# Softmax row bookkeeping per four heads instead of two, factor product on GpSimd, value products released by the copied outputs

## The chip, the cores and the metric

The kernel runs on one core of one Trainium2 chip. The metric is the device time of one execution in microseconds (us). The core's engines are TensorE (PE: matmuls and transposes, with PEld for its weight loads), VectorE (DVE), ScalarE (ACT), GpSimd (POOL) and SyncE (SP), which here issues every DMA. Each engine works through its own queue in order. Semaphores join them.

## The reference

```python
h = jnp.maximum(_layernorm(x, axis=-1), 0.0)          # x: (32, 256, 512) f32
q, k, v = (split_heads(h @ W.T) for W in (Wq, Wk, Wv))  # 16 heads of 32
a = jnp.einsum('bhnd,bhmd->bhnm', q, k) * scale + (adj + adj)[:, None]
row_nonzero = jnp.any(a != 0, axis=-1, keepdims=True)
a = jnp.where(row_nonzero, a, -jnp.inf)
p = jax.nn.softmax(a, axis=-1)
p = jnp.where(jnp.isnan(p), 0.0, p)                   # a row of zeros gives 0
o = jnp.einsum('bhnm,bhmd->bhnd', p, v)
out = x + o.transpose(0, 2, 1, 3).reshape(B, N, D) @ Wo.T
```

A row of scores that is zero throughout gives an output of zero, and all others are divided by their sum of exponentials. The "row bookkeeping" of the title is that test, the reciprocal of the sum, the product of both (the factor) and the multiplication of the head's output by it.

## The kernel before

The 32 batches are worked through one after another: `body` is written out for batch 0 and the last one, and a hardware loop does batches 1 to 30. Within a batch every engine runs over the 16 heads `hh`, in its own hand-written order, and everything is in split precision (a high and a low part).

A head `hh` passes through these steps:

- `scores` (PE, L395) writes 256 rows by 256 columns into one of three PSUM banks, three heads ahead.
- `shift` (DVE, L765) adds the adjacency, turns the sign, writes `minus` and gathers each row's bound in the last column of `bounds`. It runs two heads ahead.
- `exponentials` (ACT, L586) writes `probs`. `transpose_probs` (PE, L406) turns them. `high_probs` (ACT, L597) and `low_probs` (DVE, L774) write the two halves `pT_hi` and `pT_lo`.
- `values` (PE, L427 and L428) multiplies them with `v_parts` into the single bank `o_ps`: two heads share it, and at every even `hh` PE does both heads of the pair before. One column of ones in `v_parts` gives the row sums.

The row bookkeeping goes by pairs of heads:

- `fold` (POOL, L912 and L918) adds the halves of `minus` twice, to 64 columns a row in `bounds`, so that DVE's reduction is short.
- `any_nonzero` (DVE, at every odd `hh`, for the pair before): a reduction over `bounds` (`some`, L783) and the reciprocal of the sums, in the bank `o_ps` itself (L787).
- `factors` (DVE, L796): the factor, from `some` and `o_ps`. It stands behind the `take` calls of that head and ahead of `low_probs`.
- `copy_outputs` (ACT, L575) copies the bank to `o_raw`.
- `divide` (POOL, L887 and L892): adds the high and low outputs, and multiplies by the factor into `o`.
- `values` of the next pair waits for `factor_ready`, since the factor is read from the bank that it overwrites.

Into these steps the projections are laid as jobs (the table `JOBS`, PE L331, L346, L371). `("h", n, 1)` are the transposes of the next batch's normalised tokens (h0 at `hh` 4, h1 at 5), `("qk", n, 1)` and `("v", n, ..)` their projections, `("o", 1, -1)` at `hh` 3 the transposes of the last half of the previous batch's outputs, and `("y", n, -1)` the output projection (y0 from `hh` 4). Jobs alternate between two PSUM banks. A job starts when the job that had its bank before is "taken": copied out by ACT (high part) and DVE (low part), L551 to L564 and L729 to L747.

What stands around the change in a batch: at `hh` 0 DVE does `moments_of(b + 1)` (L665, L670) behind `low_probs`. At `hh` 1 its order is `shift` of head 3, `any_nonzero` and `factors` of the previous batch's last pair, `low_probs` of head 1. At `hh` 1 POOL's order is

```python
fold(b, 1, ...)           # waits for shift of head 3
divide(b - 1, PAIRS - 1)  # the previous batch's last pair
normalise(b + 1, False)   # L867, L869, L872, L880; then h_ready
```

and the transposes h0 at `hh` 4 wait for `h_ready` in PE's queue, with the job y0 behind them. The transposes o1 at `hh` 3 wait for `o_ready`, which `divide` gives. SP stores `y` and loads the next tokens and the adjacency, and copies `qk_parts` to `qk_stack`.

Of the kernel before, what the change touches and what calls it, by code (L numbers as in the profile page):

```python
# [5 lines left out]
ALU = mybir.AluOpType  # L6
# [7 lines left out]
P = 128  # L14
# [62 lines left out]
def attention_block(nc, x, adj, wq, wk, wv, wo_t, out):  # L77
# [9 lines left out]
    ONES, LOW = HD, HD + 1  # L87
    FREE = 3 * HD
    PAIRS = HEADS // 2

    UNTOP = 1.0 / (W_TOP * H_TOP)
# [9 lines left out]
    with ExitStack() as ctx:  # L101
# [40 lines left out]
        fold1 = [sb(f"fold1_{i}", [P, 2 * NT, N // 2]) for i in range(2)]  # L142
        some = [sb(f"some{i}", [P, 2 * NT]) for i in range(2)]
        factor = [sb(f"factor{i}", [P, 2 * NT]) for i in range(2)]

        o_raw = [sb(f"o_raw{i}", [P, 2 * NT, VW - 1]) for i in range(2)]
        probs = [sb(f"probs{i}", [P, NT, N]) for i in range(2)]
# [21 lines left out]
        o_ps = psum("o_ps")  # L169
        o_sums = o_ps[:, :].rearrange("p (q c) -> p q c", c=P)  # L170
        job_ps = [psum(f"job_ps{i}") for i in range(2)] + [s_ps[0]]
# [29 lines left out]
        some_ready, rcp_ready = sem("some_ready"), sem("rcp_ready")  # L201
        factor_ready, o_ready = sem("factor_ready"), sem("o_ready")
        o_added = sem("o_added")
# [109 lines left out]
        def _(pe):  # L313
# [23 lines left out]
            def job(kind, n, d, start, stop, b):  # L337
# [28 lines left out]
                elif kind == "o":  # L366

                    if start == 0:
                        pe.wait_ge(o_ready, (b + d) * PAIRS + 4 * (n + 1))
                    for k, t in [divmod(i, NT) for i in range(start, stop)]:  # L370
# [39 lines left out]
            def values(b, hh, early):  # L410
# [92 lines left out]
        def _(act):  # L503
# [125 lines left out]
            def body(b, first, last):  # L629
                for hh in range(HEADS):  # L630
                    if hh % 2:

                        if hh > 1:
                            copy_outputs(b, hh // 2 - 1, first and hh < 7)
                        elif not first:
                            copy_outputs(b - 1, PAIRS - 1, False)
# [23 lines left out]
        def _(dve):  # L660
# [88 lines left out]

            def shift(b, hh, early):  # L750
# [28 lines left out]

            def any_nonzero(b, pair):  # L780

                dve.wait_ge(folded2, b * PAIRS + (pair + 1))
                nc.vector.tensor_reduce(some[pair % 2][:, :], bounds[:, pair % 4, :, :], AX_X, ALU.max,  # L783
                                        apply_absolute_value=True).then_inc(some_ready, 1)

                dve.wait_ge(o_copied, b * PAIRS + (pair + 1))
                nc.vector.reciprocal(o_sums[:, :, FREE], o_sums[:, :, ONES]).then_inc(rcp_ready, 1)  # L787

            def factors(b, pair, early):

                dve.wait_ge(some_ready, b * PAIRS + (pair + 1))
                dve.wait_ge(rcp_ready, b * PAIRS + (pair + 1))
                if not early:

                    dve.wait_ge(o_ready, b * PAIRS + (pair - 1))
# [31 lines left out]
            def body(b, first, last):  # L827
                for hh in range(HEADS):
                    if hh + 2 < HEADS:
                        shift(b, hh + 2, first and hh + 2 < 4)  # L830
                    elif not last:
                        shift(b + 1, hh + 2 - HEADS, False)

                    pair = None
                    if hh % 2 and not (first and hh == 1):
                        pair = (b, hh // 2 - 1) if hh > 1 else (b - 1, PAIRS - 1)
                        any_nonzero(*pair)
                    for kind, n, d in ended_before(hh, first, last):
                        take(kind, n, b + d)
                    if pair:  # L840
                        factors(*pair, first and hh < 6)
# [7 lines left out]
            body(B - 1, False, True)  # L849
            any_nonzero(B - 1, PAIRS - 1)  # L850
            factors(B - 1, PAIRS - 1, False)
            take("o", 1, B - 1)

        @block.gpsimd
        def _(pool):
# [27 lines left out]

            def divide(b, pair):

                pool.wait_ge(factor_ready, b * PAIRS + (pair + 1))
                nc.gpsimd.tensor_tensor(o_raw[pair % 2][:, :, 0:HD], o_raw[pair % 2][:, :, 0:HD],  # L887
                                        o_raw[pair % 2][:, :, LOW:LOW + HD], ALU.add).then_inc(o_added, 1)

                pool.wait_ge(o_added, b * PAIRS + (pair + 1))  # L890
                col = 2 * pair * HD
                nc.gpsimd.tensor_tensor(  # L892
                    o[:, :, col:col + 2 * HD].rearrange("p t (h d) -> p h t d", h=2),
                    o_raw[pair % 2][:, :, 0:HD].rearrange("p (h t) d -> p h t d", h=2),
                    factor[pair % 2][:, :].rearrange("p (h t) -> p h t", h=2).unsqueeze(3).to_broadcast([P, 2, NT, HD]),
                    ALU.mult).then_inc(o_ready, 1)
# [9 lines left out]
            def fold(b, pair, early):  # L906
# [8 lines left out]
                if not early:  # L915

                    pool.wait_ge(some_ready, b * PAIRS + (pair - 1))
                nc.gpsimd.tensor_tensor(f2, f1[:, :, 0:N // 4], f1[:, :, N // 4:N // 2],  # L918
# [34 lines left out]
            def body(b, first, last):  # L953
                for hh in range(HEADS):
                    if hh % 2 == 1:
                        if hh + 2 < HEADS:
                            fold(b, hh // 2 + 1, first and hh // 2 + 1 < 2)
# [17 lines left out]
            body(B - 1, False, True)  # L975
            divide(B - 1, PAIRS - 1)
            for t in range(NT):
# [28 lines left out]
```

## Time and profile before

| | |
|---|---|
| median of 3 runs | 1286.47 us (1285.94 to 1288.19) |
| the profiled execution | 1286.69 us, span 1284.9 us |
| busy: PE, PEld | 1246.0 us (97%), 1110.2 us (86%) |
| busy: DVE, ACT, POOL | 1111.5 us (87%), 1052.2 us (82%), 898.3 us (70%) |
| mean granted TensorE clock | 0.994 of full speed |

The span runs from the first to the last instruction of the profiled execution. The busy times are sums over it. PE's matmuls are pipelined, so that the time printed for one is longer than the distance from its start to the next one's; a wait of PE is read from those distances and from the idle time printed for PEld. A batch repeats itself nearly to the nanosecond, so one batch in the middle of the span shows what all of the loop do.

### The profile page before, as it was taken

The page shows a single profiled execution, that of the slowest core. Times are in us where ns is not written, and L with a number is a line of the kernel's source. Part 1 is how long each engine was busy: PE and PEld are TensorE (multiplying, and loading weights), DVE is VectorE, ACT ScalarE, POOL GpSimd, SP SyncE. Part 2 cuts the span into 40 slices and gives each one's busy share as a digit, 9 for nine tenths or more (in the row PEclk, how much of TensorE's full clock was granted, in tenths as well). Part 3 has the DMA queues.
Part 4 walks back from the last instruction along what each step waited for, and adds up shares of the span by engine and source line. Part 5 has one row for each costly group of instructions (what it writes and reads, how often), then busy time and mean ns, then how long its engine had stood idle before and what let it go on. Part 6 is the DMA issues. An engine that isn't in the chain of part 4 may idle for free. (4 is left out here: it accounts for less than half of the span.)

```text
span 1284.9 us, 43970 instructions
## 1 busy us (share of the span) xinstructions
PE 1246.0 (97%) x13104; PEld 1110.2 (86%) x13104; DVE 1111.5 (87%) x4003; ACT 1052.2 (82%) x2429; POOL 898.3 (70%) x1272
## 2 busy tenths in 40 slices
PE   4899999999999999999999999999999999999996
PEld 4788988888988888888888888888888888988885
DVE  5798888888888888888888888888889898889884
ACT  4788888888888888888888888888888888888884
POOL 6676677776677776677776677776677776677765
PEclk9999999999999999999999999999999999999998
DMA  6344554554554554554554554554554554554551
GB/s 216 96 110 126 135 123 126 135 143 112 137 122 124 137 140 113 139 122 122 139 134 117 141 122 120 141 132 116 144 122 117 144 131 115 147 122 115 130 123 51
DMA packets 90772, 163.88 MB, mean 128 GB/s; under 512 B 14976, under 2 KB 23168, under 8 KB 90752
## 3 DMA queue, kind: packets, MB, share of 16 engines
q1 hardware_dynamic: 90752, 163.64, 49.1%
q8 instruction: 10, 0.16, 0.1%
q14 instruction: 10, 0.08, 0.0%
HBM read 46.14 MB, written 16.78 MB: 49 GB/s over the span
## 5 line engine op out<-in xcount | busy, mean ns | idle before, releaser
L912 POOL TENSOR_TENSOR fold<-minus 128x512 f32<-128x512 f32 x256 | 326.9, 1277 | 299.2 <-DVE bounds L765 299.2
L586 ACT ACTIVATE probs<-minus,bounds 128x256 f32<-128x256 f32 x1024 | 459.8, 499 | 26.6 <-DVE bounds L765 25.0
L774 DVE TENSOR_TENSOR pT_lo<-pT_ps,pT_hi 128x512 f16<-128x512 f32 x512 | 351.2, 686 | 63.2 <-ACT pT_hi L597 60.0
L765 DVE CUSTOM_DVE_ANT_0 minus<-s_ps,adj_now 128x256 f32<-128x256 f32 x1024 | 388.6, 416 | 7.7 <-ACT probs L586 4.7
L597 ACT ACTIVATE pT_hi<-pT_ps 128x512 f16<-128x512 f32 x512 | 304.9, 596 | 109.6 <-PE pT_ps L406 107.9
L406 PE MATMUL pT_ps<-ident,probs 128*128 128x128 f32 x2048 | 307.5, 273 | 1.7 <-ACT probs L586 1.6
L331 PE MATMUL job_ps<-hT_hi,w_hi 128*128 128x256 f16 x1024 | 280.5, 274 | 0.8 <-DVE hT_lo L729 0.8
L331 PE MATMUL job_ps<-hT_hi,w_lo 128*128 128x256 f16 x1024 | 279.2, 273 | 0.0
L331 PE MATMUL job_ps<-hT_lo,w_hi 128*128 128x256 f16 x1024 | 279.1, 273 | 0.0
L406 PEld LDWEIGHTS pT_ps<-ident,probs 128*128 128x128 f32 x2048 | 241.8, 141 | 19.0 <-ACT probs L586 2.5
L395 PE MATMUL s_ps<-qk_stack 96*128 96x256 f32 x1024 | 246.8, 323 | 0.0
L918 POOL TENSOR_TENSOR bounds<-fold 128x256 f32<-128x256 f32 x256 | 187.8, 734 | 24.9 <-POOL fold L912 9.5
L427 PE MATMUL o_ps<-v_parts,pT_hi 128*128 128x65 f16 x2048 | 157.1, 192 | 8.2 <-DVE pT_lo L774 7.7
L395 PEld LDWEIGHTS s_ps<-qk_stack 96*128 96x128 f32 x1024 | 154.6, 191 | 0.3 <-DMA qk_stack<-qk_parts 0.2
L428 PE MATMUL o_ps<-v_parts,pT_lo 128*128 128x33 f16 x2048 | 150.2, 178 | 0.0
L427 PEld LDWEIGHTS o_ps<-v_parts,pT_hi 128*128 128x128 f16 x2048 | 123.8, 97 | 24.0 <-DVE pT_lo L774 11.6
L331 PE MATMUL job_ps<-w_hi,hT_hi 128*128 128x256 f16 x512 | 140.7, 275 | 1.8 <-DVE qk_parts L737 1.8
L331 PE MATMUL job_ps<-w_lo,hT_hi 128*128 128x256 f16 x512 | 139.8, 273 | 0.0
L331 PE MATMUL job_ps<-w_hi,hT_lo 128*128 128x256 f16 x512 | 139.6, 273 | 0.0
L428 PEld LDWEIGHTS o_ps<-v_parts,pT_lo 128*128 128x128 f16 x2048 | 126.8, 96 | 0.0
L892 POOL TENSOR_TENSOR o<-o_raw,factor 128x128 f32<-128x128 f32 x256 | 103.1, 403 | 20.1
L331 PEld LDWEIGHTS job_ps<-hT_hi,w_hi 128*128 128x128 f16 x1024 | 99.8, 97 | 16.0 <-issue 0.9
(79 smaller groups left out, 2264.3 us busy)
## 6 DMA issues: line engine op xcount, KB each, us to landing
qk_stack<-qk_parts SPq DMA_DIRECT2D x768, 128.0 KB, 2.3
x_in<-x SPq DMA_DIRECT2D x32, 512.0 KB, 3.4
x_res<-x SPq DMA_DIRECT2D x32, 512.0 KB, 3.7
out<-y SPq DMA_DIRECT2D x64, 256.0 KB, 2.1
adj_in<-adj SPq DMA_DIRECT2D x32, 256.0 KB, 3.5
w_in<-wq SPq DMA_DIRECT2D x2, 512.0 KB, 6.1
w_in<-wk SPq DMA_DIRECT2D x2, 512.0 KB, 7.9
w_in<-wv SPq DMA_DIRECT2D x2, 512.0 KB, 9.9
```

The costliest lines, as they stand in the source:

```text
L331: end = nc.tensor.matmul(dst, lhs[a](k), rhs[c](k), start=i == 0, stop=i == len(terms) - 1)
L395: end = nc.tensor.matmul(s_ps[SCORE_BANK[hh]][:, t * N:(t + 1) * N], stack[:, 0, t * P:(t + 1) * P], stack[:, 1, :], start=True, stop=True)
L406: end = nc.tensor.transpose(pT_ps[hh % 2][:, m * N + t * P:m * N + (t + 1) * P], probs[hh % 2][:, t, m * P:(m + 1) * P], ident[:, :])
L427: nc.tensor.matmul(ps[:, 0:LOW + HD], hi, v[:, 0:LOW + HD], start=m == 0, stop=False)
L428: end = nc.tensor.matmul(ps[:, 0:HD + 1], lo, v[:, 0:HD + 1], start=False, stop=m == NT - 1)
L586: end = nc.scalar.activation(probs[hh % 2][:, t, :], minus[hh // 2 % 2][:, hh % 2, t, :], ACT.Exp, bias=bounds[:, hh // 2 % 4, 2 * (hh % 2 ...
L597: nc.scalar.activation(pT_hi[hh % 4][:, :, :], pT_ps[hh % 2][:, :].rearrange("p (m n) -> p m n", m=NT), ACT.Copy).then_inc(pT_high, 1)
L765: end = nc.vector.tensor_tensor_reduce(out=minus[pair % 2][:, hh % 2, t, :], in0=s_ps[SCORE_BANK[hh]][:, t * N:(t + 1) * N], in1=adj_now[: ...
L774: nc.vector.tensor_tensor(pT_lo[hh % 4][:, :, :], pT_ps[hh % 2][:, :].rearrange("p (m n) -> p m n", m=NT), pT_hi[hh % 4][:, :, :], ALU.sub ...
L892: nc.gpsimd.tensor_tensor(o[:, :, col:col + 2 * HD].rearrange("p t (h d) -> p h t d", h=2), o_raw[pair % 2][:, :, 0:HD].rearrange("p (h t) ...
L912: nc.gpsimd.tensor_tensor(f1[:, :, :], src[:, :, 0:N // 2], src[:, :, N // 2:N], ALU.add).then_inc(folded1, 1)
L918: nc.gpsimd.tensor_tensor(f2, f1[:, :, 0:N // 4], f1[:, :, N // 4:N // 2], ALU.add).then_inc(folded2, 1)
```

## The change

The bookkeeping goes by four heads (a "quad"). `any_nonzero` runs at `hh` 1, 5, 9 and 13: one reduction over the four heads' bounds and one reciprocal, read from `o_raw` in SBUF and written to a tile of its own. `factors` is gone from DVE. GpSimd's `divide`, at the same four `hh`, turns `some` into a mask, multiplies it with the reciprocals, adds the high and low outputs of four heads and multiplies them by the factor: four instructions for four heads, where four of the old ones served them too. `values` waits for `o_copied` instead of `factor_ready`. Semaphore counts follow, and `shift` has one wait more at every fourth head.

```diff
-        factor = [sb(f"factor{i}", [P, 2 * NT]) for i in range(2)]
-        o_raw = [sb(f"o_raw{i}", [P, 2 * NT, VW - 1]) for i in range(2)]
+        row_scale = [sb(f"row_scale{i}", [P, 4 * NT]) for i in range(2)]
+        mask = sb("mask", [P, 4 * NT])
+        factor = sb("factor", [P, 4 * NT])
+        o_raw = [sb(f"o_raw{i}", [P, 2, 2 * NT, VW - 1]) for i in range(2)]
 # PE: job "o", values
-                        pe.wait_ge(o_ready, (b + d) * PAIRS + 4 * (n + 1))
+                        pe.wait_ge(o_ready, (b + d) * QUADS + 2 * (n + 1))
-                    pe.wait_ge(factor_ready, b * PAIRS + hh // 2)
+                    pe.wait_ge(o_copied, b * PAIRS + hh // 2)
 # ACT: copy_outputs
-                    act.wait_ge(o_ready, b * PAIRS + (pair - 1))
-                nc.scalar.activation(o_raw[pair % 2][:, :, :],
+                    act.wait_ge(o_ready, b * QUADS + (pair // 2 - 1))
+                nc.scalar.activation(o_raw[pair // 2 % 2][:, pair % 2, :, :],
 # DVE: shift
+                    if hh % 4 == 0 and not fresh:
+                        dve.wait_ge(some_ready, b * QUADS + (pair // 2 - 1))
 # DVE
-            def any_nonzero(b, pair):
-                dve.wait_ge(folded2, b * PAIRS + (pair + 1))
-                nc.vector.tensor_reduce(some[pair % 2][:, :], bounds[:, pair % 4, :, :], AX_X, ALU.max, ...)
-                dve.wait_ge(o_copied, b * PAIRS + (pair + 1))
-                nc.vector.reciprocal(o_sums[:, :, FREE], o_sums[:, :, ONES]).then_inc(rcp_ready, 1)
-            def factors(b, pair, early):
...
-                nc.vector.scalar_tensor_tensor(factor[pair % 2][:, :], some[pair % 2][:, :], 0.0,
-                                               o_sums[:, :, FREE], ALU.not_equal, ALU.mult).then_inc(factor_ready, 1)
+            def any_nonzero(b, quad, early=False):
+                dve.wait_ge(folded2, b * PAIRS + 2 * (quad + 1))
+                if not early:
+                    dve.wait_ge(factor_ready, b * QUADS + (quad - 1))
+                nc.vector.tensor_reduce(some[quad % 2][:, :], bounds[:, 2 * (quad % 2):2 * (quad % 2) + 2, :, :].rearrange(
+                    "p r q c -> p (r q) c"), AX_X, ALU.max, apply_absolute_value=True).then_inc(some_ready, 1)
+                dve.wait_ge(o_copied, b * PAIRS + 2 * (quad + 1))
+                nc.vector.reciprocal(row_scale[quad % 2][:, :], o_raw[quad % 2][:, :, :, ONES]...).then_inc(rcp_ready, 1)
 # DVE: body
-                    if hh % 2 and not (first and hh == 1):
+                    if hh % 4 == 1 and not (first and hh == 1):
 # POOL
-            def divide(b, pair):
...
+            def divide(b, quad):
+                pool.wait_ge(some_ready, b * QUADS + (quad + 1))
+                settled(pool, "pool")
+                nc.gpsimd.tensor_scalar(mask[:, :], some[quad % 2][:, :], 0.0, 1.0, ALU.is_gt, ALU.mult
+                                        ).then_inc(masked, 1)
+                pool.wait_ge(masked, b * QUADS + (quad + 1))
+                pool.wait_ge(rcp_ready, b * QUADS + (quad + 1))
+                nc.gpsimd.tensor_tensor(factor[:, :], mask[:, :], row_scale[quad % 2][:, :], ALU.mult
+                                        ).then_inc(factor_ready, 1)
+                raw = o_raw[quad % 2]
+                nc.gpsimd.tensor_tensor(raw[:, :, :, 0:HD], raw[:, :, :, 0:HD], raw[:, :, :, LOW:LOW + HD],
+                                        ALU.add).then_inc(o_added, 1)
+                pool.wait_ge(factor_ready, b * QUADS + (quad + 1))
+                pool.wait_ge(o_added, b * QUADS + (quad + 1))
+                nc.gpsimd.tensor_tensor(o[...four heads...], raw[...], factor[...].to_broadcast([P, 4, NT, HD]),
+                    ALU.mult).then_inc(o_ready, 1)
 # POOL: body
-                        if hh > 1:
-                            divide(b, hh // 2 - 1)
-                        elif not first:
-                            divide(b - 1, PAIRS - 1)
+                        if hh in (5, 9, 13):
+                            divide(b, hh // 4 - 1)
+                        elif hh == 1 and not first:
+                            divide(b - 1, QUADS - 1)
```

## Rows read from the trace of the kernel before

**Rows 1.** The page, part 1: busy us, share of the span, instructions.
```profile
PE 1246.0 (97%) x13104; PEld 1110.2 (86%) x13104; DVE 1111.5 (87%) x4003; ACT 1052.2 (82%) x2429; POOL 898.3 (70%) x1272
```

**Rows 2.** The waits of PEld: total us, times, longest us.
```profile
PEld o_ps L427 <- DVE pT_lo L774: 11.6, 36, 1.0
PEld job_ps L331 <- DVE qk_parts L737: 8.4, 32, 1.7
PEld job_ps L331 <- DVE oT_lo L747: 8.0, 33, 1.8
PEld job_ps L371 <- issue: 6.2, 30, 0.2
```

**Rows 3.** The timeline of PE and PEld, heads 2 to 4: start us, us.
```profile
585.91 0.20 PE L427 MATMUL o_ps<-v_parts,pT_hi 128*128 128x65 f16 x1 [0.20 <-DVE pT_lo L774]
...
624.11 0.19 PE L427 MATMUL o_ps<-v_parts,pT_hi 128*128 128x65 f16 x1
624.52 0.20 PE L427 MATMUL o_ps<-v_parts,pT_hi 128*128 128x65 f16 x1 [0.20 <-DVE pT_lo L774]
...
627.83 0.27 PE L331 MATMUL job_ps<-w_hi,hT_lo 128*128 128x256 f16 x1
628.04 0.65 PE L371 MATMUL job_ps<-ident,o 128*128 128x128 f32 x4
629.72 0.65 PE L346 MATMUL job_ps<-ident,h 128*128 128x128 f32 x4
...
630.31 0.19 PEld L331 LDWEIGHTS job_ps<-wo_hi,oT_hi 128*128 128x128 f32 x1 [0.18 <-DVE oT_lo L747]
```

**Rows 4.** The timeline of DVE in the same batch.
```profile
620.54 1.27 DVE L665 BATCH_NORM_STATS2 stats<-x_in 128x6 f32<-128x512 f32 x2
...
622.95 0.42 DVE L783 TENSOR_REDUCE some<-bounds 128x4 f32<-128x260 f32 x1
623.29 0.18 DVE L787 RECIPROCAL o_ps<-o_ps 128x4 f32<-128x4 f32 x1
...
623.77 0.69 DVE L774 TENSOR_TENSOR pT_lo<-pT_ps,pT_hi 128x512 f16<-128x512 f32 x1
...
627.41 0.18 DVE L787 RECIPROCAL o_ps<-o_ps 128x4 f32<-128x4 f32 x1
627.50 0.41 DVE L743 SCALAR_TENSOR_TENSOR v_parts<-job_ps,v_parts 128x256 f16<-128x256 f32 x1
...
629.51 0.68 DVE L747 TENSOR_TENSOR oT_lo<-job_ps,oT_hi 128x512 fp32r<-128x512 f32 x1
```

**Rows 5.** The timeline of ACT there.
```profile
628.73 0.60 ACT L564 ACTIVATE oT_hi<-job_ps 128x512 fp32r<-128x512 f32 x1 [0.16 <-PE job_ps L371]
```

**Rows 6.** The timeline of POOL there, from the fold at head 1.
```profile
623.11 1.27 POOL L912 TENSOR_TENSOR fold<-minus 128x512 f32<-128x512 f32 x1 [2.95 <-DVE bounds L765]
624.46 0.72 POOL L918 TENSOR_TENSOR bounds<-fold 128x256 f32<-128x256 f32 x1
625.14 0.41 POOL L887 TENSOR_TENSOR o_raw<-o_raw 128x128 f32<-128x128 f32 x1
...
626.12 0.23 POOL L867 TENSOR_SCALAR minus_mean<-mean_var 128x2 f32<-128x2 f32 x1
...
627.73 1.52 POOL L880 TENSOR_SCALAR h<-x_in,minus_mean,rstd 128x512 f32<-128x512 f32 x2 [0.30 <-POOL rstd L872]
```

**Rows 7.** Groups of instructions by line: busy us, mean ns, idle before.
```profile
L892 POOL TENSOR_TENSOR o<-o_raw,factor 128x128 f32<-128x128 f32 x256 | 103.1, 403 | 20.1
...
L796 DVE SCALAR_TENSOR_TENSOR factor<-some,o_ps 128x4 f32<-128x4 f32 x256 | 39.0, 152 | 18.8 <-DVE o_ps L787 5.9
...
L677 DVE TENSOR_REDUCE w_scale<-w_in 128x2 f32<-128x1024 f32 x3 | 3.6, 1208 | 2.0 <-DMA w_in<-wk 2.0
```

**Rows 8.** The chain that ended last: start us, us, what.
```profile
1271.27 0.20 DVE o_ps L787
...
1272.73 1.13 PE s_ps L371 x4
```

More of the change, by code:

```diff
@@ L87, in attention_block @@
     ONES, LOW = HD, HD + 1
-    FREE = 3 * HD
     PAIRS = HEADS // 2
+    QUADS = HEADS // 4
     UNTOP = 1.0 / (W_TOP * H_TOP)
@@ L142, in attention_block @@
         fold1 = [sb(f"fold1_{i}", [P, 2 * NT, N // 2]) for i in range(2)]
-        some = [sb(f"some{i}", [P, 2 * NT]) for i in range(2)]
-        factor = [sb(f"factor{i}", [P, 2 * NT]) for i in range(2)]
-        o_raw = [sb(f"o_raw{i}", [P, 2 * NT, VW - 1]) for i in range(2)]
+        some = [sb(f"some{i}", [P, 4 * NT]) for i in range(2)]
+        row_scale = [sb(f"row_scale{i}", [P, 4 * NT]) for i in range(2)]
+        mask = sb("mask", [P, 4 * NT])
+        factor = sb("factor", [P, 4 * NT])
+        o_raw = [sb(f"o_raw{i}", [P, 2, 2 * NT, VW - 1]) for i in range(2)]
         probs = [sb(f"probs{i}", [P, NT, N]) for i in range(2)]
@@ L169, in attention_block @@
         o_ps = psum("o_ps")
-        o_sums = o_ps[:, :].rearrange("p (q c) -> p q c", c=P)
         job_ps = [psum(f"job_ps{i}") for i in range(2)] + [s_ps[0]]
@@ L201, in attention_block @@
         some_ready, rcp_ready = sem("some_ready"), sem("rcp_ready")
-        factor_ready, o_ready = sem("factor_ready"), sem("o_ready")
+        masked, factor_ready, o_ready = sem("masked"), sem("factor_ready"), sem("o_ready")
         o_added = sem("o_added")
@@ L633, in body @@
                         if hh > 1:
-                            copy_outputs(b, hh // 2 - 1, first and hh < 7)
+                            copy_outputs(b, hh // 2 - 1, first and hh < 10)
                         elif not first:
@@ L748, in take, with shift @@
                                             oT_hi[:, 2 * n:2 * n + 2, :].bitcast(F32), ALU.subtract).then_inc(taken["o"], 1)
-            def shift(b, hh, early):
+            def shift(b, hh, early, fresh=False):
                 pair = hh // 2
@@ L775, in low_probs @@
                                         pT_hi[hh % 4][:, :, :], ALU.subtract).then_inc(pT_split, 1)
-            def any_nonzero(b, pair):
-                dve.wait_ge(folded2, b * PAIRS + (pair + 1))
-                nc.vector.tensor_reduce(some[pair % 2][:, :], bounds[:, pair % 4, :, :], AX_X, ALU.max,
-                                        apply_absolute_value=True).then_inc(some_ready, 1)
-                dve.wait_ge(o_copied, b * PAIRS + (pair + 1))
-                nc.vector.reciprocal(o_sums[:, :, FREE], o_sums[:, :, ONES]).then_inc(rcp_ready, 1)
-            def factors(b, pair, early):
-                dve.wait_ge(some_ready, b * PAIRS + (pair + 1))
-                dve.wait_ge(rcp_ready, b * PAIRS + (pair + 1))
-                if not early:
-                    dve.wait_ge(o_ready, b * PAIRS + (pair - 1))
-                nc.vector.scalar_tensor_tensor(factor[pair % 2][:, :], some[pair % 2][:, :], 0.0,
-                                               o_sums[:, :, FREE], ALU.not_equal, ALU.mult).then_inc(factor_ready, 1)
+            def any_nonzero(b, quad, early=False):
+                dve.wait_ge(folded2, b * PAIRS + 2 * (quad + 1))
+                if not early:
+                    dve.wait_ge(factor_ready, b * QUADS + (quad - 1))
+                nc.vector.tensor_reduce(some[quad % 2][:, :], bounds[:, 2 * (quad % 2):2 * (quad % 2) + 2, :, :].rearrange(
+                    "p r q c -> p (r q) c"), AX_X, ALU.max, apply_absolute_value=True).then_inc(some_ready, 1)
+                dve.wait_ge(o_copied, b * PAIRS + 2 * (quad + 1))
+                nc.vector.reciprocal(row_scale[quad % 2][:, :], o_raw[quad % 2][:, :, :, ONES].rearrange("p r q -> p (r q)")
+                                     ).then_inc(rcp_ready, 1)
             moments_of(0)
@@ L829, in body @@
                     if hh + 2 < HEADS:
-                        shift(b, hh + 2, first and hh + 2 < 4)
+                        shift(b, hh + 2, first and hh + 2 < 4, first and hh + 2 < 8)
                     elif not last:
                         shift(b + 1, hh + 2 - HEADS, False)
-                    pair = None
-                    if hh % 2 and not (first and hh == 1):
-                        pair = (b, hh // 2 - 1) if hh > 1 else (b - 1, PAIRS - 1)
-                        any_nonzero(*pair)
+                    if hh % 4 == 1 and not (first and hh == 1):
+                        any_nonzero(*((b, hh // 4 - 1) if hh > 1 else (b - 1, QUADS - 1)), first and hh < 12)
                     for kind, n, d in ended_before(hh, first, last):
                         take(kind, n, b + d)
-                    if pair:
-                        factors(*pair, first and hh < 6)
                     low_probs(b, hh, first and hh < 2)
@@ L849, in _ @@
             body(B - 1, False, True)
-            any_nonzero(B - 1, PAIRS - 1)
-            factors(B - 1, PAIRS - 1, False)
+            any_nonzero(B - 1, QUADS - 1)
             take("o", 1, B - 1)
@@ L882, in normalise @@
                 end.then_inc(h_ready, 1)
-            def divide(b, pair):
[L886 to L891, printed above, removed]
+            def divide(b, quad):
[12 more added lines that the diff above has]
+                pool.wait_ge(o_added, b * QUADS + (quad + 1))
+                col = 4 * quad * HD
                 nc.gpsimd.tensor_tensor(
-                    o[:, :, col:col + 2 * HD].rearrange("p t (h d) -> p h t d", h=2),
-                    o_raw[pair % 2][:, :, 0:HD].rearrange("p (h t) d -> p h t d", h=2),
-                    factor[pair % 2][:, :].rearrange("p (h t) -> p h t", h=2).unsqueeze(3).to_broadcast([P, 2, NT, HD]),
+                    o[:, :, col:col + 4 * HD].rearrange("p t (h d) -> p h t d", h=4),
+                    raw[:, :, :, 0:HD].rearrange("p r (h t) d -> p (r h) t d", h=2),
+                    factor[:, :].rearrange("p (h t) -> p h t", h=4).unsqueeze(3).to_broadcast([P, 4, NT, HD]),
                     ALU.mult).then_inc(o_ready, 1)
@@ L915, in fold @@
                 if not early:
-                    pool.wait_ge(some_ready, b * PAIRS + (pair - 1))
+                    pool.wait_ge(some_ready, b * QUADS + (pair // 2 - 1))
                 nc.gpsimd.tensor_tensor(f2, f1[:, :, 0:N // 4], f1[:, :, N // 4:N // 2],
@@ L956, in body @@
                         if hh + 2 < HEADS:
-                            fold(b, hh // 2 + 1, first and hh // 2 + 1 < 2)
+                            fold(b, hh // 2 + 1, first and hh // 2 + 1 < 4)
                         elif not last:
                             fold(b + 1, 0, False)
-                        if hh > 1:
-                            divide(b, hh // 2 - 1)
-                        elif not first:
-                            divide(b - 1, PAIRS - 1)
+                        if hh in (5, 9, 13):
+                            divide(b, hh // 4 - 1)
+                        elif hh == 1 and not first:
+                            divide(b - 1, QUADS - 1)
                     if not last and hh == 1:
@@ L975, in _ @@
             body(B - 1, False, True)
-            divide(B - 1, PAIRS - 1)
+            divide(B - 1, QUADS - 1)
             for t in range(NT):
```

## The prediction

> **What bounds the kernel.** I read the page's busy times first. PE is busy 97% of the span, and DVE with 87% and POOL with 70% are not near it [rows 1]. So work taken from DVE or added to POOL is worth nothing in itself; it counts only where PE waits for that engine. The list of waits comes next. In the loop PEld waits in four places only, about once in each batch: for DVE's low probabilities, for the low parts of a qk job, for the low part of oT, and once more ahead of the transposes L371, which the profile calls issue [rows 2]. I then read one batch engine by engine. Batches repeat every 38.61 us (624.52 less 585.91) [rows 3], and all four places lie between heads 2 and 4 of it, right after DVE has done the next batch's moments. There DVE is late: from the moments at 620.54 on it works nearly without a gap [rows 4]. Elsewhere PE waits for nobody.
>
> Two limits count in this stretch, and the change touches both. DVE releases PE at heads 2 to 4. POOL gives h_ready, for which the transposes L346 (h0) wait at head 4. POOL's L880 starts at 627.73 and takes 1.52, so h_ready comes at 629.25 [rows 6]. PE starts the transposes at 629.72 [rows 3]. No wait is printed there, because there is none: PE comes 0.47 us after h_ready. If I allow 0.05 us for a release to reach PE (the distances between a release and its start in this trace are of that size: low probabilities end at 623.77 + 0.69 = 624.46 and PE starts at 624.52 [rows 3, 4]), POOL has 0.42 us of slack in every batch. Nothing in the list of waits shows this number. It has to be worked out.
>
> **The change on DVE.** At head 1 the reduction grows from 260 to 520 columns. A slope from the rows: 417 ns at 260 (0.42) and 1208 ns at 1024, so 1.035 ns a column [rows 4, 7], so 0.27 us more. The reciprocal stays (four columns more, from SBUF in place of PSUM; I take the same 0.18). The factor goes with its wait: reciprocal to low probabilities was 623.77 - 623.29 = 0.48 [rows 4], and behind a reciprocal that nobody waits for the next instruction starts after 0.09 (627.41 to 627.50) [rows 4]. Net at head 1: 0.27 - 0.39 = -0.12 us. PE's first wait is 624.52 - 624.11 = 0.41 for a step of about 0.06, so it is about 0.35 long [rows 3], and it shortens by 0.12. The second (qk parts) stays as it is: DVE is earlier by 0.12 and so is PE.
>
> At head 3 DVE has no bookkeeping at all any more. It loses a reduction's step, a reciprocal's 0.09 and a factor, together at least 0.42 us ahead of taking the v job (L743 at 627.50) [rows 4]. The transposes L371 start 0.21 behind the last product where the products of that job step by 0.11; I read the missing 0.10 as a wait for L743, which ends at 627.91 and has the bank that they need, although the profile names nobody [rows 3, 4]. That 0.10 goes. The wait for the low part of oT (0.18 printed [rows 3]) goes nearly whole: ACT's high part would end at 628.73 + 0.60 = 629.33, less PE's own gain of 0.22 [rows 5], and DVE, which started L747 at 629.51 [rows 4], is free by then. So DVE's relief is worth at most 0.12 + 0.10 + 0.18 = 0.40 us a batch. The rest of what DVE saves (in a quad two factors, a reciprocal and a step) lies under PE's work and is worth nothing; the same holds for PE's new wait for o_copied, an earlier event than the old one and not among PE's waits, and for the extra wait in shift, on DVE's own result of an earlier head.
>
> **The change on POOL.** The old divide at head 1 occupies POOL from 625.14 to the start of L867 at 626.12: 0.98 us [rows 6]. It had half of the work that the new one has there, because the new divide is bunched: it comes at heads 1, 5, 9, 13 and does four heads. Behind it in POOL's queue stands normalise, and for that PE waits. The new divide step by step:
>
> - extra wait ahead of the mask: 0.05, my estimate;
> - mask, 8 columns: nearest row L867, 0.23 [rows 6];
> - factor, 8 columns, two inputs, behind the mask's own result. A dependent start takes 0.08 (623.11 + 1.27 to 624.46) and at most 0.30 where several waits stand ahead (the idle time printed for L880) [rows 6]. I take 0.12, then 0.23 again for the operation. From above it is bounded by L887's row of 128 columns, 0.41 [rows 6];
> - add, 256 columns: L887's 0.41 at 128 plus 128 columns at the slope between the folds, (1.27 - 0.72) / 256 = 2.1 ns [rows 6]: 0.68, started 0.04 before its forerunner's printed end, as L887 did [rows 6];
> - dependent start 0.12, multiplication, L892's 0.403 + 0.27 = 0.67 [rows 7], and 0.08 to L867.
>
> The sum is 0.05 + 0.23 + 0.12 + 0.23 - 0.04 + 0.68 + 0.12 + 0.67 + 0.08 = 2.14 us, 1.16 more than before. From below: with no extra wait, 0.08 for both dependent starts, and a line through 0.23 at 2 columns and 0.41 at 128, which gives 0.59 and 0.58 for the wide ones, it is 1.82, or 0.84 more. From above: 0.30 for both starts, 0.41 for the factor, and twice the old price for the wide ones (0.82 and 0.81), it is 2.95, or 1.97 more. I take 1.16, since the wide instructions repeat two known ones at double length.
>
> The Trainium skill, GPSIMD Engine Reference, section 4.1 (Engine selection), speaks against this move: a two-input elementwise operation is to stay on VectorE, as GpSimd is about twice as slow. By it the factor would take twice DVE's 152 ns, some 0.30 us in place of my 0.23, and the total would be 30 x 0.07 = 2 us longer. This trace has no row of so small a product on POOL.
>
> **What PE sees.** POOL starts this stretch when shift of head 3 is done, which hangs on DVE's moments, and those on PE's last jobs of the batch before; nothing of that gets earlier. So h_ready comes 1.16 later, PE's h0 starts 1.16 - 0.42 = 0.74 us later than before, and whatever DVE gave back ahead of it (0.22) is swallowed by that wait. Behind h0, y0 no longer waits for oT (0.18), so the batch is 0.74 - 0.18 = 0.56 us longer. This happens where a divide and a normalise meet at head 1: batches 1 to 30, since batch 0 has no divide there and the last no normalise. 30 x 0.56 = 16.8 us. o1's transposes at head 3 wait for the same divide: it would end at 625.14 + 2.06 = 627.20, while PE comes at about 627.82 [rows 3, 6], so they are not stopped, but only 0.6 us are left.
>
> **The end.** After the last copy the chain was reciprocal, factor, add, multiplication, from 1271.27 to PE's start at 1272.73: 1.46 us [rows 8]. New: 0.18 + 0.07 + 0.23 - 0.04 + 0.68 + 0.12 + 0.67 + 0.05 = 1.96 (the mask is ready before). That is 0.50 more. The last batch, without moments and normalise, may win 0.2.
>
> Sum: 16.8 + 0.5 - 0.2 = +17.1 us. On the profiled execution's own 1286.69 us that is 1303.8. It stood 0.2 us above the median of the runs, so I predict **1303.6 us**.
>
> **Rivals.**
>
> - *DVE's relief decides (faster).* If POOL's divide grows by no more than the 0.42 us of slack, h_ready stays hidden and each of 31 batches wins up to 0.40: -12.4 + 0.5, about 1274.6 us. For it: all of PE's printed waits are for DVE, none for POOL. Against it: two operations of doubled width alone add 0.5. The sign turns where the growth reaches 0.42 + 0.18 = 0.60. Chance 0.09.
> - *The two cancel.* A growth within about 0.1 of those 0.60 gives 1286.5 within 2.6 us. Below my lower bound of 0.84, so only if small operations on POOL cost next to nothing. Chance 0.06.
> - *POOL is much dearer.* Starts with two waits at 0.30 and wide operations at double price: 1.97 more, 1.97 - 0.60 = 1.37 a batch, +41 us, about 1328. Then o1 waits too, but under the same delay. Anything above 1.5 I count here. Chance 0.10.
> - My forecast, growth of 0.84 to 1.5: +7 to +27 us, 1294 to 1314. Chance 0.75.
>
> Within 0.2% (2.6 us) is about what a measurement of this kernel can't tell from no change. So faster 0.09, same 0.06, slower 0.85. The range reaches a little below the lower bound and part of the way into the dear case: 1292 to 1318.
>
> **What the profile after would show.** A new PE wait at L346 on POOL's h, 30 times, of 0.9 to 1.0 us (0.74 and the 0.22 that PE came earlier). The wait of the o_ps products for low probabilities shortened by 0.12, those for oT and of L371 gone, that for the qk parts as before. DVE busy time down by some 80 us, POOL's up by about 25 (128 quads at 0.23 + 0.23 + 0.68 + 0.67 for what were two pairs of 0.41 + 0.40). A batch period of 39.17 us. Copying and exponentials as before. I am wrong if L346 shows no wait (then POOL's operations are cheaper than any row), if the wait is much longer than 1 us (the prices of small dependent operations on POOL), or if PE waits in new places at heads 5 to 15, where POOL and DVE have room by these rows.

## The result and the profile after

The changed kernel takes 1297.08 us (median of 4 runs, 1295.66 to 1298.89) against 1286.2 us before (4 runs): a ratio of 1.0086, 95% interval 1.0073 to 1.0099, or +10.9 us. Forecast was 1303.6 us, +17.1. The profiled execution took 1297.27 us, span 1295.5 us, at the same mean granted clock, 0.994.

The page, parts 1 and 4 (the chain of work that ended last, by engine and by line), answers to [rows 1]:

```profile
PE 1239.1 (96%) x13104; PEld 1111.2 (86%) x13104; DVE 1068.8 (83%) x3491; ACT 1047.3 (81%) x2429; POOL 907.6 (70%) x1272
...
issue 47%; POOL 43%; PE 5%; POOLq 2%; DVE 2%; ACT 1%; DMA 0%; DVEq 0%; ACTq 0%
POOL fold L914 15%; POOL o_raw L888 6%; POOL y L906 5%; POOL bounds L920 4%; PE job_ps L332 3%; POOL mask L881 2%; POOL o L894 2%; POOL h L873 2%; POOL factor L885 2%; POOL rstd L865 2%; POOL w_in L935 1%; PE pT_ps L407 1%; POOL minus_mean L860 1%; POOL var_eps L862 0%; POOLq L913 0%
```

DVE lost 43 us of work and POOL gained 9, yet the kernel got slower. An engine that is busy for 70% of the span has 43% of the chain, more than all other engines together; the other large share, 47%, is what the page calls issue, time in which the engine waited for nothing that the profile shows. The waits say where POOL stops PE; the four lines of [rows 2] have become

```profile
PEld job_ps L347 <- POOL h L873: 26.7, 30, 0.9
PE job_ps L347 <- POOL h L873: 23.5, 30, 0.8
...
PEld job_ps L332 <- DVE qk_parts L738: 8.4, 32, 1.7
...
PEld o_ps L428 <- DVE pT_lo L778: 5.1, 22, 1.2
...
PEld job_ps L332 <- DVE oT_lo L748: 2.5, 3, 1.6
```

The waits for DVE have gone or shrunk, all but that for the qk parts, and 30 waits for the normalised tokens are new. The timeline of PE (to [rows 3]):

```profile
591.12 0.19 PE L428 MATMUL o_ps<-v_parts,pT_hi 128*128 128x65 f16 x1
...
594.37 0.60 PE L372 MATMUL job_ps<-ident,o 128*128 128x128 f32 x4
...
595.89 0.19 PE L428 MATMUL o_ps<-v_parts,pT_hi 128*128 128x65 f16 x1
596.87 0.66 PE L347 MATMUL job_ps<-ident,h 128*128 128x128 f32 x4 [0.78 <-POOL h L873]
...
635.88 0.66 PE L347 MATMUL job_ps<-ident,h 128*128 128x128 f32 x4 [0.78 <-POOL h L873]
```

and of POOL in the same batch (to [rows 6]):

```profile
589.69 1.29 POOL L914 TENSOR_TENSOR fold<-minus 128x512 f32<-128x512 f32 x1 [3.59 <-DVE bounds L769]
591.14 0.73 POOL L920 TENSOR_TENSOR bounds<-fold 128x256 f32<-128x256 f32 x1 [0.17 <-POOL fold L914]
591.83 0.25 POOL L881 TENSOR_SCALAR mask<-some 128x8 f32<-128x8 f32 x1
592.16 0.20 POOL L885 TENSOR_TENSOR factor<-mask,row_scale 128x8 f32<-128x8 f32 x1
592.32 0.63 POOL L888 TENSOR_TENSOR o_raw<-o_raw 128x256 f32<-128x256 f32 x1
593.10 0.62 POOL L894 TENSOR_TENSOR o<-o_raw,factor 128x256 f32<-128x256 f32 x1
593.69 0.24 POOL L860 TENSOR_SCALAR minus_mean<-mean_var 128x2 f32<-128x2 f32 x1
...
594.28 0.72 POOL L865 TENSOR_TENSOR rstd<-var_eps,minus_half 128x2 f32<-128x2 f32 x1
595.30 1.52 POOL L873 TENSOR_SCALAR h<-x_in,minus_mean,rstd 128x512 f32<-128x512 f32 x2 [0.30 <-POOL rstd L865]
```

The reader can follow one fact through both. L873 ends at 595.30 + 1.52 = 596.82, and PE starts at 596.87, 0.05 later: PE now hangs on POOL directly. The next batch's h0 is at 635.88, a batch is 39.01 us long, and it was 38.61 [rows 3]. From the fold's start to the end of L873 POOL takes 7.13 us, and it took 6.14 (623.11 to 629.25) [rows 6]: 0.99 more.

On the steps of PE's stream, start to start and averaged over the 30 loop batches of each trace, the change is: ahead of values(1) 0.379 to 0.222 us; ahead of and inside the o transposes 0.145 less; ahead of h0 0.082 to 0.960; ahead of y0 0.215 to 0.028. The sum is 0.878 - 0.157 - 0.145 - 0.187 = +0.389 us a batch, times 30 is 11.7. The two spans differ by 10.6.

### The profile page after: what moved, and what is told of

Read it like the earlier page. It is cut to its first block, busy times and chain, and to the rows that moved or that the text cites. A ratio compares the mean times of both kernels' runs of the same rounds, so it can differ in the third digit from the quotient of the medians.

```text
span 1295.5 us, 43769 instructions
## 1 busy us (share of the span) xinstructions
PE 1239.1 (96%) x13104; PEld 1111.2 (86%) x13104; DVE 1068.8 (83%) x3491; ACT 1047.3 (81%) x2429; POOL 907.6 (70%) x1272
## 4 chain that ended last, share of the span: by engine, by line
issue 47%; POOL 43%; PE 5%; POOLq 2%; DVE 2%; ACT 1%; DMA 0%; DVEq 0%; ACTq 0%
POOL fold L914 15%; POOL o_raw L888 6%; POOL y L906 5%; POOL bounds L920 4%; PE job_ps L332 3%; POOL mask L881 2%; POOL o L894 2%; POOL h L873 2%; POOL factor L885 2%; POOL rstd L865 2%; POOL w_in L935 1%; PE pT_ps L407 1%; POOL minus_mean L860 1%; POOL var_eps L862 0%; POOLq L913 0%
## 5 line engine op out<-in xcount | busy, mean ns | idle before, releaser
L332 PE MATMUL job_ps<-wo_hi,oT_hi 128*128 128x512 f32 x256 | 109.9, 429 | 2.0 <-DVE oT_lo L748 2.0
```

Of the source, the lines that this page charges most:

```text
L332: end = nc.tensor.matmul(dst, lhs[a](k), rhs[c](k), start=i == 0, stop=i == len(terms) - 1)
```

## The experiments

"Period" below is the mean distance of the first transposes of one batch from those of the next over the loop, in the profiled execution (38.62 us before, 39.00 after; the 30 distances of one trace agree within 0.03 us and 0.06 us). Each time is the median, with the ratio to the kernel before on the same chip.

**Is there a slack of 0.42 us, and what comes past it?** The kernel before, with one addition on a spare tile ahead of `normalise` (and, once at the start, a memset of that tile):

```diff
                     if not last and hh == 1:
+                        if not first:
+                            pool.wait_ge(idled, 1)
+                            nc.gpsimd.tensor_tensor(idle[:, 1, 0:n], idle[:, 0, 0:n], idle[:, 0, 0:n], ALU.add)
                         normalise(b + 1, False)
```

With n = 128: 

> The kernel before, with one addition of 128 columns on POOL (on a tile of its own, which no result uses) between divide and normalise at head 1 of batches 1 to 30. Slack theory: it delays h_ready by about 0.36 to 0.40 us, less than the 0.42 us of slack that I worked out, so the batch period stays at 38.62 us and the time within 1 us of the kernel before. Rival (no slack: POOL's time at head 1 counts in full): 30 x 0.37 = +11 us.

Measured: 1286.04 us, ratio 0.9997 (0.9987 to 1.0007), period 38.63 us. h_ready came 0.35 us later, and nothing happened.

With n = 512: 

> The same with 512 columns, about 1.24 us more on POOL. Slack theory: PE's transposes h0 start 1.24 - 0.42 = 0.82 us later, and y0's wait for oT (0.19) vanishes behind them: +0.63 us a batch, +19 us in all, about 1305 us. Rival (POOL's queue at head 1 does not reach PE, and the slowdown after the change came from PE's new wait or DVE's longer reduction): 0. Rival (full price): +37 us.

Measured: 1295.85 us, ratio 1.0076 (1.0059 to 1.0093), period 39.00 us. The expectation was missed because of the addition's price, not the mechanism: with one tile as both inputs it took 1.04 us in place of 1.24.

```profile
629.73 1.04 POOL L970 TENSOR_TENSOR idle<-idle 128x512 f32<-128x512 f32 x1
630.84 0.23 POOL L870 TENSOR_SCALAR minus_mean<-mean_var 128x2 f32<-128x2 f32 x1
...
632.44 1.52 POOL L883 TENSOR_SCALAR h<-x_in,minus_mean,rstd 128x512 f32<-128x512 f32 x2 [0.30 <-POOL rstd L875]
```

It delayed h_ready by 0.98 us on the mean of the loop, by chance within 0.01 of the changed kernel's own figure. In the batch of these rows h_ready stands at 11.65 us and h0 at 11.70 us behind the batch's first transposes, and both figures are the same, within 0.01, in the changed kernel's batch. PE's h0 moved by 0.56, which leaves 0.42 of slack. So a delay on POOL of the change's size, put into a kernel whose loop is otherwise untouched, costs 9.7 us, nearly the whole of the 10.9. By 0.98 - 0.42 - 0.19 the sum gives 0.37 a batch, and the period grew by 0.38.

**Does the loss go when h comes earlier?** `normalise` is cut in two, and its three small instructions stand ahead of the fold, where POOL was idle for 3.59 us:

```diff
+                    if not last and hh == 1:
+                        prepare(b + 1)            # minus_mean, var_eps, rstd
                     if hh % 2 == 1:
                         ... fold, divide ...
                     if not last and hh == 1:
-                        normalise(b + 1, False)   # all four
+                        normalise(b + 1, False)   # h alone
```

In the changed kernel: 

> The changed kernel, with normalise's three small instructions (minus_mean, var_eps, rstd) put ahead of fold at head 1, where POOL had been idle. Theory: they need only the moments, ready 0.9 us before the fold can start, so about 0.8 us of their 1.6 us moves into idle time; h_ready comes about 0.8 us earlier, PE's wait for h (0.88 us a batch) shrinks to 0.1 or less, and what DVE gave back (0.49 us a batch) shows. o_ready comes 0.83 us later and may stop the o transposes at head 3 by about 0.2 us. Period 38.1 to 38.35 us against 38.62 before: about 1277 us (1272 to 1280), faster than the kernel before. Rival (the loss is PE's new wait or DVE's longer reduction): no better than the changed kernel's 1297.

Measured: 1277.14 us, ratio 0.9936 (0.9913 to 0.996), period 38.36 us. PE's wait for h is gone, and 30 waits for o (at most 0.2 us) stand ahead of the o transposes instead.

In the kernel before: 

> The kernel before with the same move of normalise's three small instructions ahead of fold. Theory: there PE does not wait for h, so an h_ready 0.8 us earlier is worth nothing; o_ready comes 0.8 us later, at about 8.3 us of the batch, where PE wants it at 9.4. Period 38.62 us, time within 2 us of the kernel before. Rival (the move is a gain of its own, whatever the rest): 5 us or more faster.

Measured: 1285.93 us, ratio 0.9996 (0.9986 to 1.0006), period 38.63 us. The same edit is worth some 20 us in one kernel and nothing in the other, because only in one of them does PE wait for h.

**Is it the added instructions or the doubled ones?** The factor back on DVE, as one instruction for four heads:

```diff
 # DVE, behind low_probs at heads 1, 5, 9, 13
+                nc.vector.scalar_tensor_tensor(factor[quad % 2][:, :], some[quad % 2][:, :], 0.0,
+                                               row_scale[quad % 2][:, :], ALU.not_equal, ALU.mult)
 # POOL, divide: no mask, no factor; it waits for o_copied and, ahead of the multiplication, for factor_ready
```

> The changed kernel with the factor of four heads made by one instruction on DVE, behind low_probs at heads 1, 5, 9 and 13, and no mask and no factor on POOL. Theory: POOL's divide gets shorter by the 0.49 us from mask to add, PE's wait for h falls from 0.88 to about 0.4 us, DVE pays some 0.08 us a quad: period 39.00 - 0.49 + 0.05 = 38.56 us, about 1284 us, a shade faster than the kernel before. If moving the factor is not what costs, but the bunching of two pairs' add and multiplication alone, it stays near 1297.

Measured: 1285.54 us, ratio 0.9997 (0.9985 to 1.001), period 38.61 us. The step ahead of h0 fell from 0.960 to 0.457, by the 0.49 of those two instructions, and the step ahead of the second v job grew by 0.11.

The first pair's addition ahead of time:

```diff
+                        if hh % 4 == 3:
+                            add_first(b, hh // 4)   # 128 columns: L888's first half; divide adds the second
```

> The changed kernel with only the first pair's low part added ahead, at heads 3, 7, 11 and 15. Theory: divide at head 1 is 0.22 us shorter, and PE waits for h 0.22 us less: period 39.00 - 0.22 = 38.78 us, about 1290.5 us. Rival (the two small instructions and their waits are what costs, not the doubled width): no change from 1297.

Measured: 1286.85 us, ratio 1.0007 (0.9996 to 1.0019), period 38.69 us. The step ahead of h0 fell by 0.30, not 0.22: the addition of half the width takes 0.41 in place of 0.63, and the multiplication behind it starts 0.08 after its end, where it was 0.14 in the changed kernel. Both parts of the longer divide count, each with its own length.

**What is PE's new wait worth?**

```diff
+                    if hh % 4 == 0:
+                        pe.wait_ge(factor_ready, b * QUADS + hh // 4)
                     pe.wait_ge(o_copied, b * PAIRS + hh // 2)
```

> The changed kernel, but value products at every fourth head wait for factor_ready too, as they did before. At head 2 of a batch PE wants to start them 5.34 us after the batch's start, and POOL has the factor of the last quad at 7.19. Theory: PE loses about 1.9 us there; its later waits (0.20 for low probabilities, 0.09 for the qk parts, 0.88 for h) vanish behind it, so that the period grows from 39.00 to about 39.75 us: about 1320 us (1315 to 1326). Rival: the factor of a quad is off PE's path, and the new wait is of no use: 1297.

Measured: 1375.26 us, ratio 1.0685 (1.0667 to 1.0702), period 41.50 us.

```profile
PEld o_ps L430 <- issue: 106.6, 93, 2.3
PE o_ps L430 <- POOL factor L887: 87.5, 61, 2.1
```

The direction was right and the size far off. I had looked at head 2 alone; there PE lost 2.20 us, but it lost 0.97 at head 10 and 0.23 at head 14 too. A smaller part is the clock. The mean granted clock fell to 0.984 from 0.994, and five of the 30 loop batches, every fifth to seventh, are 1.65 us longer than the others (42.87 in place of 41.22 us), some 8 us in all. In each of the five, and in no other loop batch, the trace has a stretch of 3.4 us at a granted clock of 0.5 (the 1.2 GHz level). It begins 0.9 to 1.5 us after PE's wait at head 2 has ended. Here are two batches in a row, and then the same stretch of each (start and end in us; the third number from the end is the granted clock):

```profile
290.00:332.80 42.80, 39.85 (x410) 35.42 (x408) 33.14 (x108) 32.57 (x75) 27.63 (x39) 0.96 0.45 115
332.80:374.10 41.30, 38.37 (x411) 34.42 (x410) 33.03 (x108) 32.47 (x76) 27.75 (x40) 1.00 0.46 121
298.80:302.20 3.40, 3.40 (x18) 2.78 (x16) 0.99 (x2) 2.16 (x6) 3.02 (x5) 0.51 0.88 198
341.60:345.00 3.40, 3.40 (x33) 3.19 (x30) 1.93 (x7) 3.05 (x8) 2.95 (x5) 1.00 0.86 195
```

Why the clock falls in these five and not in the others, which have the same wait, stays open. What stands is that a factor on POOL is only affordable with the wait on o_copied.

**The fastest version.** Small instructions and first addition early, together: 

> The changed kernel with the small instructions of normalise ahead of the fold and, besides, the first pair's low part added at heads 3, 7, 11 and 15, so that divide adds one pair only. Theory: o_ready comes 0.22 us earlier than with the first alone, the o transposes (at 9.32 us of the batch there, 9.20 without a wait) are released in time, h is ready before PE comes, and all of DVE's relief shows: 0.16 + 0.15 + up to 0.19 us. Period 38.12 to 38.25 us, about 1272 us (1270 to 1275). Rival (a further wait takes its place at once, DVE or ACT): 1277 as with the first alone.

Measured: 1273.05 us, ratio 0.9901 (0.9884 to 0.9917), period 38.17 us: 13.1 us less than before, 24 less than the changed kernel. The timelines of POOL and PE there:

```profile
615.43 0.24 POOL L860 TENSOR_SCALAR minus_mean<-mean_var 128x2 f32<-128x2 f32 x1 [2.72 <-DVE mean_var L671]
...
616.71 1.28 POOL L924 TENSOR_TENSOR fold<-minus 128x512 f32<-128x512 f32 x1
...
619.96 0.62 POOL L904 TENSOR_TENSOR o<-o_raw,factor 128x256 f32<-128x256 f32 x1
620.57 1.54 POOL L876 TENSOR_SCALAR h<-x_in,minus_mean,rstd 128x512 f32<-128x512 f32 x2
```
```profile
622.38 0.63 PE L347 MATMUL job_ps<-ident,h 128*128 128x128 f32 x4
```

h is ready at 622.11, PE comes at 622.38 and waits for nobody.

**A third edit that should have been free.** The factor on DVE on top of it: 

> The same, and the factor of four heads on DVE behind low_probs in place of mask and factor on POOL. Theory: with h no longer waited for, POOL's 0.49 us are worth nothing, and DVE's extra instruction costs the 0.11 us a batch that it cost ahead of the v job when tried alone: period 38.25 to 38.35 us, about 1275 us, 3 us slower than without it. Rival (POOL is still the limit): faster than without it.

Measured: 1292.45 us, ratio 1.0042 (1.0028 to 1.0056), period 38.86 us: not 3 but 19 us slower. The step ahead of the second v job had grown by 0.68 us. DVE's and POOL's timelines show why:

```profile
631.74 0.75 DVE L803 SCALAR_TENSOR_TENSOR factor<-some,row_scale 128x8 f32<-128x8 f32 x1
632.41 0.41 DVE L768 CUSTOM_DVE_ANT_0 minus<-s_ps,adj_now 128x256 f32<-128x256 f32 x1
```
```profile
631.19 1.28 POOL L930 TENSOR_TENSOR fold<-minus 128x512 f32<-128x512 f32 x1
```

Eight columns take 0.75 us and end at 632.49; POOL's fold ends at 632.47. All 128 factors of this kernel end 22 to 47 ns after the end of a POOL instruction, and take 0.156 to 0.765 us to get there. The same instruction in the kernel with the factor on DVE alone took 0.19 us at head 1, because there it started 0.16 us ahead of the fold's end. Three runs put an instruction of 8 columns whose result nobody uses at the same place of the 1273 us kernel.

```diff
 # DVE, behind low_probs at heads 1, 5, 9, 13
+                nc.vector.scalar_tensor_tensor(probe, some, 0.0, row_scale, ALU.not_equal, ALU.mult)  # two inputs
+                nc.vector.tensor_scalar(probe, some, 0.0, 1.0, ALU.is_gt, ALU.mult)                   # one input
+                nc.vector.reciprocal(probe, row_scale)                                                # reciprocal
```

> The fastest kernel so far (small instructions and first addition early, 1273 us), with one more DVE instruction of 8 columns behind low_probs at heads 1, 5, 9 and 13, whose result nobody uses: the one that made the factor on DVE, with both inputs (some, row_scale) in SBUF. New theory: a DVE instruction with two SBUF inputs does not finish before the instruction that POOL is in ends. At head 1 POOL is in the fold (5.10 to 6.38 us of the batch), so it takes about 0.75 us instead of 0.16, PE's wait ahead of the second v job grows by about 0.68 us, period 38.86 us, about 1293 us. Rival (the third kernel of that kind was slow for another reason, such as a wait for o_ready or the later fold): within 4 us of 1273.

Measured: 1292.08 us, ratio 1.0054 (1.0035 to 1.0073), period 38.87 us, as expected.

> The same place, waits and size, but an instruction with one SBUF input (some alone). New theory: it does not wait for POOL, takes about 0.15 us, and delays the second v job by about 0.1 us: period 38.25 to 38.3 us, about 1276 us. Rival (the place behind low_probs or its waits are what costs, whatever the inputs): 1293 like the other.

Measured: 1292.22 us, ratio 1.0051 (1.0035 to 1.0068), period 38.87 us: the expectation failed, and with it the theory that two SBUF inputs are what counts.

```profile
626.68 0.76 DVE L802 TENSOR_SCALAR probe<-some 128x8 f32<-128x8 f32 x1
```
```profile
626.14 1.27 POOL L933 TENSOR_TENSOR fold<-minus 128x512 f32<-128x512 f32 x1
```

> The same place, waits and size a third time, with a reciprocal of row_scale as the extra instruction. In the changed kernel the reciprocal (one SBUF input, SBUF output, 8 columns) took 0.19 us each time although POOL was busy at its start nearly always, while the product (two SBUF inputs) and tensor_scalar (one) both ended within 60 ns after a POOL instruction's end nearly always. Theory as it now stands: what counts is whether the instruction uses the SBUF ports that DVE and POOL share; product and tensor_scalar do, the reciprocal does not. So it takes about 0.2 us, the second v job waits about 0.1 us more than in the 1273 us kernel: period 38.25 to 38.3 us, about 1276 us. Rival (any extra instruction behind low_probs at that place stands until the fold ends, through its waits or the order of the queue): 1292 like the other two.

Measured: 1275.23 us, ratio 0.9913 (0.9891 to 0.9936), period 38.28 us.

```profile
618.93 0.20 DVE L802 RECIPROCAL probe<-row_scale 128x8 f32<-128x8 f32 x1
```
```profile
618.39 1.27 POOL L933 TENSOR_TENSOR fold<-minus 128x512 f32<-128x512 f32 x1
```

The reciprocal starts in the middle of the same fold and takes 0.20 us. So neither the place nor the waits are what costs, but the kind of instruction. The expectation said "nearly always" too freely: in the changed kernel the reciprocal began inside a POOL instruction in 97 of 128 cases, and 96 of the 127 two-input instructions ended within 60 ns after a POOL instruction, as did 125 of the 127 with one input. In the run above the reciprocal took 0.190 to 0.197 us in all 127 cases, and began inside a POOL instruction in 126 of them.

## Why the prediction was right, and what it mis-sized

**The bound.** That PE waits for DVE between heads 2 and 4 only held, and so, to the hundredth, did the 0.42 us of slack on POOL, which no view prints. The spare additions, which delayed h_ready by 0.35 us (no cost) and 0.98 us (+9.7 us), lie on both sides of it.

**DVE's relief.** Forecast 0.12 + 0.10 + 0.18 us a batch. The first two measured 0.157 and 0.145. In the changed kernel the third, the wait of y0 for the low part of oT, fell by 0.187, but that is not DVE's doing: it fell by as much in the kernel before with 512 spare columns, where DVE was as late as ever and h0 came 0.56 us later. A late h0 hides this wait, as the sum had it. What DVE's relief is worth at this place is seen in the 1273 us kernel, where nothing covers it: 0.054 ahead of y0 and 0.074 ahead of and inside the h transposes, 0.13 together in place of 0.18. The wait for the qk parts stayed as it was, as said. The missing 0.10 ahead of the o transposes, which the profile calls issue, was DVE's v job: it went when that came earlier. In all the 1273 us kernel's period is 0.45 us shorter than before, where I had put the relief at 0.40 at most.

**POOL's divide.** This is the term that was mis-sized. I took 1.16 us more ahead of h_ready; it was 0.99. The divide itself grew by 0.88 (from L887's start to L867's, 0.98, to L881's start to L860's, 1.86), next to my lower bound of 0.84 (its terms add up to 1.83 and so to 0.85, and those of the upper bound to 2.96 and 1.98; I had each 0.01 lower). The wide instructions took 0.63 and 0.62 where I took 0.68 and 0.67; the factor 0.20 where I took 0.23; the starts behind a result 0.08 to 0.15, the mask started without the extra 0.05. A line through the two-column and the 128-column rows, my lower bound, would have been the better estimate. In the other direction the second fold starts 0.10 later behind the first than before, since a register instruction for its changed count now stands in between. I had no term for that. By my own rule 0.99 - 0.42 - 0.19 gives 0.38 a batch, and 0.389 was measured by the four steps, 0.384 by the periods. So this term, mis-sized by 0.17 us a batch, is 5.1 of the 6.2 us between forecast and measurement; most of the rest is at the ends.

**Busy times.** I had DVE down by some 80 us and POOL up by about 25; it was 43 and 9 [rows 1]. POOL's miss is the prices above: its groups by line add up to 10 us more than before. For DVE I had added up printed durations, but neighbours on one engine overlap by some 0.05 to 0.1 us (a reciprocal of 0.18 adds 0.09 [rows 4]), so removing an instruction removes less than its duration. This did not enter the sum, which goes by starts.

**The end.** From the last copy to the o transposes I had 0.50 us more; the step ahead of them grew by 0.49. The last batch won more than my 0.2: its waits for low probabilities at heads 8 to 12 shrank by 0.75 us in sum. The granted clock differs at the ends of the two profiled executions: its mean was 0.91 and then 0.94 from the last batch's first transposes on, and 1.00 and then 0.95 in batch 0. That made the end about 0.9 us shorter. Batch 0 took 0.8 us longer, and how much of this is the clock is not shown; the 30 loop batches, and with them the sum's main term, are not touched.

**The rivals.** *DVE's relief decides* was wrong for this kernel but names what the edit could have been: it takes only a POOL order that hides the divide. *The two cancel* is what a shorter divide gives: both kernels with 0.3 to 0.5 us less on POOL stand at 1286. Nothing speaks for *POOL is much dearer*. A rule that I had weighed, the Trainium skill's GPSIMD Engine Reference, section 4.1, would have put the factor at 0.30 us by my estimate. It took 0.20 on POOL, against 0.15 for four columns on DVE, so for so small an operation the factor of two does not show.

**The change to PE's wait** I had costed at nothing. That is right as far as time goes, yet the move of the factor to POOL rests on it: without it the kernel takes 1375 us.

## What to carry to other kernels

Batching small work saves instructions but makes the batch that runs longer, and what counts is who stands behind it in the queue at that moment: here `normalise`, at one of four places. Before such an edit, work out for each release to the bounding engine how long before its use it comes. That slack is printed nowhere, and a spare instruction that is longer than the slack measures it in one run: here h_ready came 0.98 us later, PE 0.56. If the slack is too small, look for instructions behind the longer block whose inputs are ready ahead of it, and move them in front.

## What the runs showed of the hardware

A small DVE instruction can stand until POOL's current instruction ends. With both inputs in SBUF (scalar_tensor_tensor), and with one input and an output there (tensor_scalar), 8 columns took 0.16 to 0.9 us, and about 0.76 in the middle of a fold; the reciprocal of 8 columns from SBUF to SBUF took 0.190 to 0.197 at the same places. The groups by line of the three kernels:

```profile
L802 DVE SCALAR_TENSOR_TENSOR probe<-some,row_scale 128x8 f32<-128x8 f32 x127 | 47.3, 373 | 0.0
```
```profile
L802 DVE TENSOR_SCALAR probe<-some 128x8 f32<-128x8 f32 x127 | 49.1, 386 | 0.0
```
```profile
L802 DVE RECIPROCAL probe<-row_scale 128x8 f32<-128x8 f32 x127 | 24.5, 193 | 0.0
```

The Trainium skill, SBUF — State Buffer, section "Who interferes with whom", says that VectorE and GpSimd share a pair of SBUF ports as an exclusive lock, held for a whole instruction, and that VectorE contends for it with two SBUF inputs, when GpSimd's instruction reads SBUF, or in a mode that uses two ports on one tensor. The Trainium skill, Advanced Engine Details and Errata, section VectorE Performance Modes, gives as that mode's conditions that source and destination lie in SBUF and that the count is even in both, as with tensor_scalar over 8 columns; its list of instructions has tensor_scalar and not the reciprocal. The waits behind the fold (0.76 us against 0.19 for the reciprocal) agree with this. That the mode was on in the one-input run is my reading; no row prints it. One thing does not fit: at head 5 the two-input instruction began 0.06 to 0.09 us behind the printed start of POOL's mask and took 0.16 us, as little as with nothing in its way. It did so in all 30 loop batches and mostly ended ahead of the mask, where the one-input instruction at the same place ended 0.02 to 0.03 us behind the mask (0.19 us). Why stays open.

The kernel before kept clear of this: its factor took its second input from a PSUM bank [rows 7], and no factor there took more than 0.159 us, although POOL was busy at the start of 254 of the 256. And POOL's additions of 256 columns took 0.734 us over two stretches of `fold1` but 0.632 over `o_raw`, so its price is not one line over the number of columns.
